# Paged keys turned by VectorE and pages gathered by SyncE in a two-layer attention kernel

## The chip, the cores and the metric

The kernel runs on one core of one Trainium2 chip. The metric is the device time of one execution in microseconds (us), here the median of three runs.

## The reference

Eight sequences (B=8) of 128 tokens, width 512, go through four residual steps. Layer 0: a windowed attention on x times an adapter matrix chosen by sequence, then a routed low-rank network. Layer 1: attention 1, causal with an alibi bias, on gated x; then attention 2 on the result, with a paged key and value cache, and a quantised two-matrix network on its output. What matters is attention 2:

```python
kc = k_cache[block_table].reshape(bsz, L, HK, D)      # 16 pages of 32 tokens, L=512
vc = v_cache[block_table].reshape(bsz, L, HK, D)
k_all = jnp.concatenate([kc, k], axis=1)              # k: normed and rotated, own 128 tokens
v_all = jnp.concatenate([vc, v], axis=1)
scores = jnp.einsum('bqhd,bkhd->bhqk', q, k_all) * SCALE
scores = jnp.where(valid[:, None, None, :], scores, -1e+30)
probs = jax.nn.softmax(scores, axis=-1)
o = jnp.einsum('bhqk,bkhd->bqhd', probs, v_all)
return jnp.einsum('bse,de->bsd', o.reshape(bsz, seqlen, HQ * D), Wo)
...
h = _dyn_quant_linear(_layernorm(attn2, gamma, beta), w1, b1)   # rows to 127 steps
out = x + _dyn_quant_linear(gelu(h), w3, b3)
```

There are 32 query heads in 8 key/value groups, head width 128; block_table and the cache lengths are inputs. All is float32; the cache holds 64 pages of 32 tokens x 8 groups x 128.

## The kernel before

Every engine's order is written out by hand, and semaphores tie the engines. Layer 0 goes sequence by sequence. Each attention of layer 1 has 64 items (ITEMS): for each of 8 groups g (four query heads, one key/value head) the 8 sequences b. Float32 products are done as three products of a high and a low part: ScalarE copies the high part (rounded), VectorE or GpSimd subtracts to get the low.

An item of attention 2 (step(i) of each engine). TensorE: scores of four heads (L1629, L1632) into two-bank pairs, the next item's key and value projection (project_kv, L1580), the transposes of the next item's four cached key tiles (turn_cached_k, L1589, bank 3), the output projection of the item before (project_out, L1674), the five transposed probability chunks (turn_probs, L1647) and their products with the values (weigh, L1662), and between them in quarters the query projection of the item after next (project_q, L1566), and the turned queries and key of the next (L1598, L1604). VectorE: four row maxima from the scores (row_max, L1991), the low part of the output (lo_of_o, L2013), two normalisations, the rotation of the next item's queries (spread_q, L1935 to L1939, and join_q, L1945) and key, then low parts of probabilities (L2007), cached keys (lo_of_cached_k, L1976), queries and key. ScalarE: exponentials, high parts, the squares of the query projection (q_squares, L2344). GpSimd: low part of the cached values (L2531), norm factors, and eight indirect DMAs per item, four 128x128 tiles of keys (L2517) and four of values (L2525), with row numbers made at the start (dve_positions, rows).

project_out of an item waits for the four row maxima of the next and for lo_of_o; row_max(0) frees bank 0 for the scores of head 3. Items with b=0 also split output weights (L1927), those with b=5 and b=6 the next group's query, key and value weights (L1922).

SyncE's queue (sp_layer0, sp_attentions) issues all other loads in order: in layer 0 one adapter per sequence, in attention 1 for each g the query/key/value weights, the output weights, in g=3 to 6 two stores of finished quantised weights (keep_units), and in g=2 to 5 two loads of rows of the quantised network's weights (load_units, L1322). VectorE takes those rows (unit_steps, L1895) as the first thing after the row maxima of items 10, 12, 18, 20, 26, 28, 34 and 36 (UNIT_ITEM), both loads of a pair being waited for at the first:

```python
            def unit_steps(n):
                dve.wait_ge(s_wn, 32 * (n // 2 + 1))
                row_steps(unit_step[:, n:n + 1], unit_inv[:, n:n + 1], unit_rows[n % 2])
```

After item 56 (LAST) the quantised network of each finished sequence is worked into the last items; quantised_end does the rest.

## Time and profile before

| | |
|---|---|
| median of 3 runs | 2039.4 us (2039.14 to 2040.28) |
| profiled execution | 2048.39 us, its span 2046.6 us |
| TensorE busy | 1990.2 us, 97% |
| VectorE busy | 1533.6 us, 75% |
| ScalarE busy | 1323.5 us, 65% |
| GpSimd busy | 801.8 us, 39%, of it 507.1 in 512 indirect DMAs (976 and 1005 ns each) |
| mean granted TensorE clock | 0.995 of full speed |

Layer 0 goes to about 300 us, attention 1 to 890 us, attention 2 to 2018 us, the rest is the quantised end. Busy time of TensorE overstates its work, as its products are pipelined; the starts of its instructions are what to read. The profiled execution is one run, longer than the median by 9.0 us.

### The profile page before, as it was taken

The page shows a single profiled execution, that of the slowest core. Times are in us where ns is not written, and L with a number is a line of the kernel's source. Part 1 is how long each engine was busy: PE and PEld are TensorE (multiplying, and loading weights), DVE is VectorE, ACT ScalarE, POOL GpSimd, SP SyncE. Part 2 cuts the span into 40 slices and gives each one's busy share as a digit, 9 for nine tenths or more (in the row PEclk, how much of TensorE's full clock was granted, in tenths as well). Part 3 has the DMA queues.
Part 4 walks back from the last instruction along what each step waited for, and adds up shares of the span by engine and source line. Part 5 has one row for each costly group of instructions (what it writes and reads, how often), then busy time and mean ns, then how long its engine had stood idle before and what let it go on. Part 6 is the DMA issues. An engine that isn't in the chain of part 4 may idle for free.

```text
span 2046.6 us, 35827 instructions
## 1 busy us (share of the span) xinstructions
PE 1990.2 (97%) x12449; PEld 1696.5 (83%) x12456; DVE 1533.6 (75%) x3383; ACT 1323.5 (65%) x3796; POOL 801.8 (39%) x797
## 2 busy tenths in 40 slices
PE   6999999999999999999999999999999999999986
PEld 5778677888888888888888888888888888888873
DVE  6777764556666555687887888878878888888997
ACT  4676763545554554566776777767767777677785
POOL 3200015100000000056666666666666666666662
PEclk9999999999999999999999999999999999999998
DMA  7301101101201110121111111211111111112000
GB/s 259 98 28 48 53 1 73 62 32 37 68 32 51 43 53 1 58 78 32 62 53 31 62 51 31 82 32 53 61 32 62 53 32 63 53 32 83 26 28 36
DMA packets 45010, 108.60 MB, mean 53 GB/s; under 512 B 15634, under 2 KB 21010, under 8 KB 40354
## 3 DMA queue, kind: packets, MB, share of 16 engines
q1 hardware_dynamic: 28450, 72.74, 10.3%
q0 software_dynamic: 16384, 33.59, 5.6%
q8 instruction: 102, 1.67, 0.3%
q14 instruction: 74, 0.61, 0.1%
HBM read 103.14 MB, written 3.15 MB: 52 GB/s over the span
## 4 chain that ended last, share of the span: by engine, by line
PE 90%; DVE 5%; ACT 3%; issue 1%; DMA 1%; SPq 0%; DVEq 0%; ACTq 0%
PE PS L1662 10%; PE PS L1487 9%; PE PS L1430 9%; PE PS L1674 8%; PE PS L1566 8%; PE PS L1629 7%; PE PS L1647 7%; PE PS L1580 4%; PE PS L1443 4%; PE PS L1632 3%; PE PS L342 3%; PE PS L1458 3%; PE PS L1473 2%; PE PS L498 1%; PE PS L1465 1%; PE PS L1589 1%
## 5 line engine op out<-in xcount | busy, mean ns | idle before, releaser
L2517 POOL DMA_INDIRECT kcache<-in_kcache,rows x256 | 249.9, 976 | 533.4 <-DVE x_res L1818 462.4
L2525 POOL DMA_INDIRECT vcache<-in_vcache,rows x256 | 257.2, 1005 | 124.2 <-issue 58.4
L1991 DVE CUSTOM_DVE_ANT_0 pr<-PS,ffn_weights,sm 128x640 f32<-128x640 f32 x256 | 224.6, 885 | 88.6 <-PE PS L1632 88.6
L2007 DVE TENSOR_TENSOR prT_lo<-PS,prT_hi 128x512 fp32r<-128x512 f32 x320 | 209.2, 685 | 46.1 <-ACT prT_hi L2387 41.8
L2376 ACT ACTIVATE pr<-pr,sm 128x640 f32<-128x640 f32 x256 | 212.3, 831 | 40.1 <-DVE sm L1991 40.0
L2387 ACT ACTIVATE prT_hi<-PS 128x512 fp32r<-128x512 f32 x320 | 178.9, 597 | 78.5 <-PE PS L1647 67.3
L1647 PE MATMUL PS<-consts,pr 128*128 128x128 f32 x1280 | 174.0, 273 | 2.7 <-DVE prT_lo L2007 1.6
L1647 PEld LDWEIGHTS PS<-consts,pr 128*128 128x128 f32 x1280 | 149.7, 141 | 28.8 <-issue 3.7
L2531 POOL TENSOR_TENSOR vcached_lo<-vcache,vcached_hi 128x512 fp32r<-128x512 f32 x64 | 83.2, 1300 | 228.8 <-ACT vcached_hi L2359 228.6
L1629 PE MATMUL PS<-kT_hi,qT_hi 128*128 128x320 f32 x512 | 154.5, 310 | 2.2 <-DVE sm L1991 1.3
L1629 PE MATMUL PS<-kT_lo,qT_hi 128*128 128x320 f32 x512 | 154.1, 309 | 0.0
L2381 ACT ACTIVATE pr<-pr,sm 128x640 f32<-128x640 f32 x128 | 99.3, 824 | 29.1 <-issue 25.8
L1566 PE MATMUL PS<-w_qkv_hi,xT_hi 128*128 128x512 f32 x256 | 117.5, 459 | 0.0
L1632 PE MATMUL PS<-kT_hi,qT_lo 128*128 128x320 f32 x512 | 116.6, 309 | 0.0
L2255 ACT ACTIVATE oT_hi<-PS 128x512 fp32r<-128x512 f32 x64 | 38.2, 597 | 116.7 <-PE PS L1473 116.7
L1430 PE MATMUL PS<-xT_hi,w_qkv_hi 128*128 128x512 f32 x256 | 110.4, 431 | 0.9 <-DVE xT_lo L1777 0.6
L1662 PE MATMUL PS<-prT_hi,vcached_hi 128*128 128x512 f32 x256 | 108.1, 422 | 2.8 <-DVE prT_lo L2007 2.1
L1674 PE MATMUL PS<-w_out_hi,oT_hi 128*128 128x512 f32 x256 | 106.8, 417 | 3.4 <-DVE oT_lo L2013 3.3
L2244 ACT ACTIVATE pr<-pr,sm 128x128 f32<-128x128 f32 x256 | 99.1, 392 | 6.1 <-DVE sm L1804 6.1
L1487 PE MATMUL PS<-w_out_hi,oT_hi 128*128 128x512 f32 x256 | 101.9, 398 | 0.2 <-DVE oT_lo L1832 0.2
L1629 PEld LDWEIGHTS PS<-kT_hi,qT_hi 128*128 128x128 f32 x512 | 96.1, 188 | 6.8 <-issue 2.5
L1566 PE MATMUL PS<-w_qkv_hi,xT_lo 128*128 128x512 f32 x256 | 101.4, 396 | 0.0
(319 smaller groups left out, 6173.3 us busy)
## 6 DMA issues: line engine op xcount, KB each, us to landing
arena<-in_wqkv SPq DMA_DIRECT2D x16, 1536.0 KB, 6.3
arena<-in_wo SPq DMA_DIRECT2D x16, 1024.0 KB, 5.4
arena<-in_wcT SPq DMA_DIRECT2D x8, 1024.0 KB, 6.6
kcache<-in_kcache,rows POOLq DMA_INDIRECT x256
vcache<-in_vcache,rows POOLq DMA_INDIRECT x256
arena<-in_xT SPq DMA_DIRECT2D x8, 256.0 KB, 8.2
x_res<-in_x SPq DMA_DIRECT2D x1, 2048.0 KB, 13.4
ffn_weights<-in_alibi SPq DMA_DIRECT2D x2, 1024.0 KB, 6.9
```

Of the source, the lines that this page charges most:

```text
L1430: mm = pe.matmul(bank(HEAD_BANK[n] if n < 2 * GH else 1), w_qkv[c][:, k, r * P:(r + 1) * P], (x_hi, x_lo)[a][:, k, GH * half:GH * (half + ...
L1487: mm = pe.matmul(bank(0 if last else 5), o2[a][:, h, :], w_out[c][:, h, :], start=(h == 0 and j == 0), stop=(h == GH - 1 and j == 2))
L1566: mm = pe.matmul(bank(7), (x_hi, x_lo)[a][:, k, b, :], w_qkv[c][:, k, 0:GH * HD], start=(k == 0 and j == 0), stop=(k == KT - 1 and j == 2))
L1629: pe.matmul(bank(SCORE_BANK[h] + half, HALF), qT2[0][:, h, :], kT2[c][:, half * HALF:(half + 1) * HALF], start=(c == 0), stop=False)
L1647: mm = pe.transpose(bank(4 + n % 2, P, h * P), pr2[:, h, c * P:(c + 1) * P], ident)
L1662: mm = pe.matmul(bank(6), v[a], prT2[e][:, n % 3, :, :].rearrange("p h n -> p (h n)"), start=(c == 0 and j == 0), stop=(c == CHUNKS and j ...
L1674: mm = pe.matmul(bank(0), o2[a][:, h, :], w_out[c][:, h, :], start=(h == 0 and j == 0), stop=(h == GH - 1 and j == 2))
L1991: dve.tensor_tensor_reduce(pr2[:, h, :].rearrange("p (a n) -> p a n", a=2), PS[:, SCORE_BANK[h]:SCORE_BANK[h] + 2, 0:HALF], keymask[:, b, ...
L2007: dve.tensor_tensor(prT2[1][:, n % 3, :, :].rearrange("p h n -> p (h n)"), bank(4 + n % 2), prT2[0][:, n % 3, :, :].rearrange("p h n -> p ...
L2376: act.activation(pr2[:, h, :], pr2[:, h, :], ACT.Exp, bias=nm2[:, h:h + 1], scale=-1.0, accum_out=rs2[:, h:h + 1]).then_inc(a2_ex, 1)
L2517: pool.indirect_dma_start(out=kcache[:, c, :], out_offset=None, in_=T["kcache"], in_offset=bass.IndirectOffsetOnAxis(ap=rows[:, g, b, c:c ...
L2525: pool.indirect_dma_start(out=vcache[:, c, :], out_offset=None, in_=T["vcache"], in_offset=bass.IndirectOffsetOnAxis(ap=rows[:, g, b, c:c ...
```

## The change

The pages of both caches are first copied, whole and in the order of the block table, into two DRAM tensors (kpages, vpages) by SyncE, one register load and two DMAs of 128 KB per page, 13 pages after each adapter of sequences 3 to 7 and 9 pages in each g=1 to 7 of attention 1. In attention 2 SyncE then loads each item's keys with four DMAs, each taking a quarter of the head width as pieces of 32 numbers, so that VectorE's transpose of 32x32 blocks gives the keys turned; values come with one DMA. TensorE's transposes of keys go. ScalarE's high part of the keys moves behind the third probability chunk, the low part goes to GpSimd. spread_q of the next item moves ahead of the row maxima, and the first quarter of the query projection ahead of the output projection. turn_hidden waits for a row maximum instead of the keys' low part. At the end sequence 6's dequantisation, steps and gelu move ahead and TensorE gets extra products that write a bank nobody reads (stay_warm). The weight loads of attention 2 are put between key and value loads. Page row numbers and positions on VectorE go; GpSimd makes the positions.

```diff
@@ -183,7 +180,7 @@
             kT2 = [sb2(f"kT2_{part}", [P, NKEY], F32R) for part in ("hi", "lo")]
-            kcache = sb2("kcache", [P, CHUNKS, HD])
+            kcache = sb2("kcache", [P, CACHED])
             vcache = sb2("vcache", [P, CHUNKS, HD])
@@ -207,6 +204,7 @@
         consts0 = area(22528, NCONST0)
+        kraw = cst["iota"]
         cst.update({n: consts0[:, a:b] for n, (a, b) in CONST0_COLS.items()})
@@ -276,9 +275,25 @@
         s_ym, s_g8 = sem("token_means"), sem("gate_ready")
-        NLOADF, NSETUP = 6, 10
+        NLOADF, NSETUP = 6, 7
...
         counted = {"dve": 0, "pool": 0}
+
+        kpages = nc.dram_tensor("gathered_k_pages", [B, SLOTS, PAGE, G, HD], F32).ap()
+        vpages = nc.dram_tensor("gathered_v_pages", [B, SLOTS, PAGE, G, HD], F32).ap()
+        L0_PAGES, A1_PAGES = 13, 9
+
+        def gather(sp, first, count):
+            if first == 0:
+                sp.wait_ge(s_setup, 16 * NSETUP)
+            for n in range(first, first + count):
+                b, s = n // SLOTS, n % SLOTS
+                at = (s % 4) * B * CHUNKS + b * CHUNKS + s // 4
+                page = sp.value_load(page_ids[0:1, at:at + 1], min_val=0, max_val=NPAGE - 1)
+                for kept, name in ((kpages, "kcache"), (vpages, "vcache")):
+                    sp.dma_start(kept[b, s:s + 1].rearrange("a t g d -> a t (g d)"),
+                                 T[name].rearrange("(a t g) d -> a t (g d)", a=NPAGE, g=G)[bass.ds(page, 1), :, :]
+                                 ).then_inc(s_gathered, 16)
@@ -314,6 +329,7 @@
                 adapter(b)
+                gather(sp, L0_PAGES * (b - 3), L0_PAGES)
@@ -1164,8 +1179,7 @@
         def sp_paged_inputs(sp):
-            for q in range(4):
-                sp.dma_start(page_i[q * 32:(q + 1) * 32, :], T["pages"][q, :].partition_broadcast(32)).then_inc(s_setup, 16)
+            sp.dma_start(page_ids[:], T["pages"].rearrange("q n -> (q n)").unsqueeze(0)).then_inc(s_setup, 16)
             sp.dma_start(clen_i[:], T["cache_len"].partition_broadcast(P)).then_inc(s_setup, 16)
@@ -1328,6 +1332,34 @@
+            def load_keys(n):
+                g, b = group_of(n)
+                if n == 0:
+                    sp.wait_ge(a2_mask, 2 * B)
+                    sp.wait_ge(a1_acc, ITEMS - B)
+                wait(sp, a2_kcT, n)
+                for j in range(4):
+                    sp.dma_start(kraw[j * PAGE:(j + 1) * PAGE, :].rearrange("t (s d) -> t s d", s=SLOTS),
+                                 kpages[b, :, :, g, j * PAGE:(j + 1) * PAGE].rearrange("s t d -> t s d")).then_inc(a2_kg, 16)
+
+            def load_values(n):
+                g, b = group_of(n)
+                if n == 0:
+                    sp.wait_ge(a1_sc, ITEMS)
+                wait(sp, a2_vcl, n)
+                sp.dma_start(vcache[:], vpages[b, :, :, g, :].rearrange("(c s) t d -> (s t) c d", c=CHUNKS)
+                             ).then_inc(a2_vg, 16)
+
+            def load_qkv_weights2(g):
+                wait(sp, a2_wl, QPARTS * g)
+                sp.dma_start(stage_qkv.rearrange("p t n -> p (t n)"),
+                             T["wqkv2"][g, :, :, :].rearrange("p t n -> p (t n)")).then_inc(a2_w, 16)
+
+            def load_out_weights2(g):
+                wait(sp, a2_wol, GH * g)
+                sp.dma_start(stage_out.rearrange("p h n -> p (h n)"),
+                             T["wo2"][g, :, :, :].rearrange("p h n -> p (h n)")).then_inc(a2_wo, 16)
+
             sp.wait_ge(s_prec, 3)
@@ -1341,6 +1373,8 @@
                     table(1)
+                if g:
+                    gather(sp, L0_PAGES * (B - 3) + A1_PAGES * (g - 1), A1_PAGES)
                 if 3 <= g < 7:
@@ -1350,23 +1384,37 @@
             sp.wait_ge(a1_wol, GH * G)
-            for g in range(G):
-                wait(sp, a2_wl, QPARTS * g)
-                sp.dma_start(stage_qkv.rearrange("p t n -> p (t n)"),
-                             T["wqkv2"][g, :, :, :].rearrange("p t n -> p (t n)")).then_inc(a2_w, 16)
-                wait(sp, a2_wol, GH * g)
-                sp.dma_start(stage_out.rearrange("p h n -> p (h n)"),
-                             T["wo2"][g, :, :, :].rearrange("p h n -> p (h n)")).then_inc(a2_wo, 16)
+            load_qkv_weights2(0)
+            load_out_weights2(0)
+            sp.wait_ge(s_gathered, 16 * 2 * B * SLOTS)
+            load_keys(0)
+            load_qkv_weights2(1)
+            load_values(0)
+            load_keys(1)
+            for i in range(LAST):
+                load_values(i + 1)
+                load_keys(i + 2)
+                g, b = group_of(i)
+                if b == 0:
+                    load_out_weights2(g + 1)
+                if b == B - 1 and g + 2 < G:
+                    load_qkv_weights2(g + 2)
...
             sp.dma_start(wrow.rearrange("p w n -> p (w n)"), step_kept.partition_broadcast(P)).then_inc(s_fi, 16)
+            load_values(LAST + 1)
+            load_keys(LAST + 2)
...
                 sp.dma_start(brow[:, w, :], T[bias].partition_broadcast(P)).then_inc(s_fi, 16)
+            for i in range(LAST + 1, ITEMS - 1):
+                load_values(i + 1)
+                if i + 2 < ITEMS:
+                    load_keys(i + 2)
@@ -1523,8 +1571,6 @@
                     project_q(0, (3,))
-                elif i == ITEMS - 2:
-                    turn_cached_k(0)
                 elif i == ITEMS - 1:
@@ -1581,14 +1627,6 @@
-            def turn_cached_k(n):
-                pe.wait_ge(a2_kg, 16 * CHUNKS * (n + 1))
-                if n == 0:
-                    pe.wait_ge(a1_kTc, ITEMS)
-                for c in range(CHUNKS):
-                    mm = pe.transpose(bank(3, P, c * P), kcache[:, c, :], ident)
-                mm.then_inc(a2_kcT, 1)
-
             def turn_q(n):
@@ -1677,9 +1717,11 @@
                 scores(i)
+                more = i + 2 < ITEMS
...
                     project_kv(i + 1)
-                    turn_cached_k(i + 1)
+                if more:
+                    project_q(i + 2, (0,))
                 if i >= 1:
@@ -1688,9 +1730,8 @@
                 turn_probs(i, 1)
-                more = i + 2 < ITEMS
                 if more:
-                    project_q(i + 2, (0, 1))
+                    project_q(i + 2, (1,))
                 if i + 1 < ITEMS:
@@ -1720,8 +1761,8 @@
                 pe.wait_ge(s_hq, n + 1)
-                if i is not None and i + 1 < ITEMS:
-                    pe.wait_ge(a2_kcl, i + 2)
+                if i is not None:
+                    pe.wait_ge(a2_max, 4 * i + 2)
                 else:
@@ -1746,6 +1787,10 @@
+            def stay_warm(n):
+                for _ in range(n):
+                    pe.matmul(bank(6), identb[:], wT16[:, 0, 0, :], start=True, stop=True)
+
             def quantised_end():
@@ -1753,12 +1798,19 @@
                 turn_hidden(5, 1)
+                stay_warm(2)
                 linear(5, 1, 4)
+                stay_warm(4)
                 turn_hidden(7, 0, bk=1)
+                stay_warm(2)
                 linear(7, 0, 0)
+                stay_warm(5)
                 turn_hidden(6, 1)
+                stay_warm(2)
                 linear(6, 1, 5)
+                stay_warm(4)
                 turn_hidden(7, 1)
+                stay_warm(2)
                 linear(7, 1, 7)
@@ -1850,6 +1902,7 @@
                     spread_q(0)
+                    turn_cached_k(0)
                 normalise1(i)
@@ -1971,9 +2019,10 @@
-            def lo_of_cached_k(n):
-                dve.wait_ge(a2_kch, n + 1)
-                dve.tensor_tensor(kT2[1][:, 0:CACHED], bank(3), kT2[0][:, 0:CACHED], ALU.subtract).then_inc(a2_kcl, 1)
+            def turn_cached_k(n):
+                dve.wait_ge(a2_kg, 16 * 4 * (n + 1))
+                wait(dve, a2_kcl, n)
+                dve.transpose(kcache[:], kraw).then_inc(a2_kcT, 1)
@@ -2026,6 +2075,8 @@
                 q = i - LAST
+                if more:
+                    spread_q(i + 1)
                 if q >= 4:
@@ -2039,7 +2090,7 @@
                 if more:
-                    rotate_q(i + 1)
+                    join_q(i + 1)
                     rotate_k(i + 1)
@@ -2049,7 +2100,7 @@
                     lo_of_own_v(i + 1)
-                    lo_of_cached_k(i + 1)
+                    turn_cached_k(i + 1)
                     norm_k(i + 1)
@@ -2167,14 +2218,14 @@
                 to_steps(5, 1)
+                dequantise1(6, 7)
...
                 quantise_hidden(7, 0)
-                dequantise1(6, 7)
+                hidden_steps(6, 1)
...
                 dequantise1(7, 0)
-                hidden_steps(6, 1)
                 hidden_steps(7, 1)
@@ -2354,14 +2405,15 @@
             def hi_of_cached_v(n):
-                act.wait_ge(a2_vg, 16 * CHUNKS * (n + 1))
+                act.wait_ge(a2_vg, 16 * (n + 1))
...
                 act.wait_ge(a2_kcT, n + 1)
-                act.activation(kT2[0][:, 0:CACHED], bank(3), ACT.Copy).then_inc(a2_kch, 1)
+                wait(act, a2_sc, 4 * n)
+                act.activation(kT2[0][:, 0:CACHED], kcache[:], ACT.Copy).then_inc(a2_kch, 1)
@@ -2414,8 +2466,6 @@
                     scale_hidden(q - 2, 0)
-                if more:
-                    hi_of_cached_k(i + 1)
                 if i + ITEMS - FROM_X < B:
@@ -2425,6 +2475,8 @@
                 hi_of_probs(i, 2)
+                if more:
+                    hi_of_cached_k(i + 1)
                 if new_out:
@@ -2491,12 +2543,12 @@
                 hidden_copy(5, 1)
+                gelu(6)
                 hidden_copy(7, 0, 1)
-                gelu(6)
-                gelu(7)
...
                 hidden_copy(6, 1)
+                gelu(7)
                 hidden_copy(7, 1)
@@ -2510,21 +2562,9 @@
-            def load_keys(n):
-                g, b = group_of(n)
-                wait(pool, a2_kcT, n)
-                for c in range(CHUNKS):
-                    pool.indirect_dma_start(out=kcache[:, c, :], out_offset=None, in_=T["kcache"],
-                                            in_offset=bass.IndirectOffsetOnAxis(ap=rows[:, g, b, c:c + 1], axis=0)
-                                            ).then_inc(a2_kg, 16)
-
-            def load_values(n, cs=range(CHUNKS)):
-                g, b = group_of(n)
-                wait(pool, a2_vcl, n)
-                for c in cs:
-                    pool.indirect_dma_start(out=vcache[:, c, :], out_offset=None, in_=T["vcache"],
-                                            in_offset=bass.IndirectOffsetOnAxis(ap=rows[:, g, b, c:c + 1], axis=0)
-                                            ).then_inc(a2_vg, 16)
+            def lo_of_cached_k(n):
+                pool.wait_ge(a2_kch, n + 1)
+                pool.tensor_tensor(kT2[1][:, 0:CACHED], kcache[:], kT2[0][:, 0:CACHED], ALU.subtract).then_inc(a2_kcl, 1)
@@ -2556,20 +2594,13 @@
-            pool.wait_ge(a1_acc, ITEMS - B)
-            load_keys(0)
-            pool.wait_ge(a1_sc, ITEMS)
-            load_values(0, (0, 1))
             factors(0)
-            load_values(0, (2, 3))
-            load_keys(1)
+            lo_of_cached_k(0)
...
                 if i + 1 < ITEMS:
-                    load_values(i + 1)
                     factors(i + 1)
-                if i + 2 < ITEMS:
-                    load_keys(i + 2)
+                    lo_of_cached_k(i + 1)
                 q = i - LAST
@@ -2577,9 +2608,13 @@
                     dequantise2(q - 4)
-                if q >= 1:
+                if q == 1:
+                    pool.wait_ge(s_fi, 16 * 6)
+                    bias_residual(7)
+                if 1 <= q < 7:
                     bias_residual(q - 1)
-            bias_residual(7)
+                if q == 6:
+                    bias_residual(6)
             root(7)
```

## Rows read from the trace of the kernel before

**Rows 1.** The page: the chain that ended last, shares of the span by engine.

```profile
PE 90%; DVE 5%; ACT 3%; issue 1%; DMA 1%; SPq 0%; DVEq 0%; ACTq 0%
```

**Rows 2.** Three items: us, then each engine's busy us (instructions), clock, DMA share, GB/s.

```profile
1272.13:1290.15 18.02, 17.86 (x105) 15.30 (x104) 16.56 (x36) 14.27 (x42) 10.36 (x11) 1.00 0.11 30
1324.48:1341.64 17.16, 17.16 (x105) 15.26 (x104) 14.37 (x34) 12.07 (x33) 10.97 (x11) 1.00 0.29 93
1934.30:1955.90 21.60, 20.01 (x120) 16.41 (x122) 19.93 (x50) 17.66 (x43) 15.34 (x15) 1.00 0.09 26
```

**Rows 3.** The chain in order of time, attention 2: start us, us, what.

```profile
1312.40 0.44 PE PS L1589 x4
```

**Rows 4.** Groups by line and shape: busy us, mean ns of one, idle before.

```profile
L1976 DVE TENSOR_TENSOR kT_lo<-PS,kT_hi 128x512 fp32r<-128x512 f32 x64 | 43.6, 681 | 0.0
...
L1922 DVE TENSOR_TENSOR w_qkv_lo<-arena,w_qkv_hi 128x1024 fp32r<-128x1024 f32 x8 | 9.8, 1225 | 2.0 <-ACT w_qkv_hi L2330 2.0
...
L2531 POOL TENSOR_TENSOR vcached_lo<-vcache,vcached_hi 128x512 fp32r<-128x512 f32 x64 | 83.2, 1300 | 228.8 <-ACT vcached_hi L2359 228.6 <-issue 0.2
```

**Rows 5.** Timeline, VectorE, items b=0: start us, us, engine, line, what [idle before].

```profile
1308.38 0.89 DVE L1991 CUSTOM_DVE_ANT_0 pr<-PS,ffn_weights,sm 128x640 f32<-128x640 f32 x1 [2.16 <-PE PS L1632]
...
1313.63 0.41 DVE L1935 TENSOR_TENSOR swapped<-PS,arena 128x256 f32<-128x256 f32 x1
...
1314.28 0.68 DVE L1939 TENSOR_TENSOR qk<-PS,arena 128x512 f32<-128x512 f32 x1
...
1323.32 1.89 DVE L1927 TENSOR_TENSOR w_out_lo<-arena,w_out_hi 128x512 fp32r<-128x512 f32 x3
```

**Rows 6.** Timeline, start of the item b=6 from 1272.13.

```profile
1273.20 0.21 ACT L2344 ACTIVATION_READ_ACCUMULATOR square<-PS 128x1 f32 x1
...
1273.21 0.89 DVE L1991 CUSTOM_DVE_ANT_0 pr<-PS,ffn_weights,sm 128x640 f32<-128x640 f32 x1
...
1276.65 0.69 DVE L2013 TENSOR_TENSOR oT_lo<-PS,oT_hi 128x512 fp32r<-128x512 f32 x1
...
1277.42 0.48 PE L1674 MATMUL PS<-w_out_hi,oT_hi 128*128 128x512 f32 x1
```

**Rows 7.** Timeline, SyncE's queue in layer 0.

```profile
25.90 2.55 SPq L309 DMA_DIRECT2D ffn_weights<-in_loraB  x1
...
61.61 0.37 SPq L314 DMA_DIRECT2D ffn_weights<-in_ffnB  x1
...
62.73 0.39 SPq L287 DMA_DIRECT2D arena<-in_wcT  x1
```

**Rows 8.** Timeline, quantisation rows loaded and used, groups g=2 and g=3.

```profile
394.51 0.91 SPq L1322 DMA_DIRECT2D arena<-in_w  x2
...
401.18 0.68 DVE L1895 TENSOR_REDUCE arena<-arena 128x1 f32<-128x512 f32 x1
...
468.85 1.56 SPq L1322 DMA_DIRECT2D arena<-in_w  x2
...
475.22 0.69 DVE L1895 TENSOR_REDUCE arena<-arena 128x1 f32<-128x512 f32 x1 [0.65 <-DMA arena<-in_w]
...
476.41 0.69 DVE L1813 TENSOR_TENSOR pr<-pr,sm 128x512 f32<-128x512 f32 x1
...
478.73 0.27 PE L1465 MATMUL PS<-consts,pr 128*128 128x128 f32 x1
```

**Rows 9.** Stretch at half clock in layer 0, columns as in rows 2.

```profile
42.41:45.82 3.41, 3.41 (x9) 2.64 (x8) 2.18 (x5) 1.94 (x4) 3.24 (x3) 0.50 0.01 2
```

**Rows 10.** Timeline, quantised end.

```profile
2037.16 0.43 DVE L2126 TENSOR_SCALAR arena<-ffn_weights 128x512 bf16<-128x512 f32 x1 [0.87 <-PE PS L1734]
...
2039.44 0.63 PE L1734 MATMUL PS<-identb,arena 128*128 128x128 bf16 x4
...
2040.76 1.89 PE L1745 MATMUL PS<-arena 128*128 128x512 bf16 x4 [0.69 <-ACT arena L2474]
```

**Rows 11.** DMA issues by line: count, KB each, median us to landing.

```profile
quantised_weights<-arena SPq DMA_DIRECT2D x8, 128.0 KB, 5.4
```

32 lines of the change are left out of this document (8 added, 24 removed).

## The prediction

> **What bounds the kernel now.** I read the page first: the span is 2046.6 us and TensorE is busy 97% of it. The chain that ended last is 90% TensorE [rows 1], so almost any instruction taken off TensorE should count, and so should any new wait of TensorE. Then I cut attention 2 into its items. The reader should see in [rows 2] that an ordinary item takes 17.16 us, with TensorE busy throughout, VectorE for 14.37 us even in an item that also splits weights, and GpSimd for 10.97. The item starts (first score product of each item) are 17.16 to 17.18 us apart in 48 of the first 57 items; seven, the seventh of each group (b=6), take 18.02, with TensorE waiting 0.8 us, and the first two are longer than that rule. The last seven items are different: the one from 1934.30 takes 21.60 us with VectorE busy 19.93 [rows 2]. There VectorE and ScalarE, with the quantised end's work between, set the pace. A measurement of this kernel can tell about 0.2% (4 us) from no change.
>
> **Cached keys.** Per item the change takes four TensorE transposes away. In the chain they cost 0.44 us, at 1312.40, between the k/v projection and the output projection [rows 3]. The 57 TensorE-bound items and the one transposed ahead in attention 1 give 58 x 0.44 = 25.5 us saved. On VectorE a subtraction of 0.681 us (128x512) leaves [rows 4] and a 32x32-block transpose of 128x512 in SBUF comes in. No row shows one. Bounds: 0.61 us (half of the 128x1024 subtraction's 1.225) and 1.225 itself, if it ran at half rate [rows 4]; I take 0.68, because the nearest row is an operation with as many elements, so VectorE's load stays. The Trainium skill (VectorE: DVE Perf Modes, section "The three transpose paths") gives 311 ns for 128x128 in bf16 and 390 ns for TensorE's; four times the first is an estimate of 1.24 us, and by it VectorE would have 0.56 us more per item, which an ordinary item's idle time holds. No row here shows a VectorE transpose to test it.
>
> The copy to kT_hi stays on ScalarE but moves behind the third probability chunk; its remainder moves to GpSimd, where the same shape takes 1.300 us [rows 4]. GpSimd loses eight indirect DMAs per item, about 1 us each, so it has room. The remainder would end some 2 us before the next item's scores: cost nothing; without that room, up to 1.3 us per item. The last seven items are bound elsewhere: I take -1.5 us for them, between -6 (the idle of VectorE filled by the query rotation) and +4 (seven transposes at 1.225).
>
> **Query rotation ahead of the row maxima.** It reads bank 7 after ScalarE's squares and takes 1.33 us (1313.63 to 1314.96) [rows 5]. In an ordinary item VectorE idles 2.16 us just there, before the row maximum at 1308.38 [rows 5], so the rotation is free, and its cover is this idle. In two items of each group the idle is gone. In the second item (b=1) VectorE is still splitting output weights until 1325.21 [rows 5]; rotation then ends at 1326.54, while the first row maximum started 1.08 us after the item's start, at 1325.56: 0.98 late. In b=6 the squares end at 1273.41 and the rotation at 1274.78, against a row maximum at 1273.21: 1.57 late [rows 6]. Who waits: the output projection, which needs all row maxima and oT_lo. It started at 1277.42; without transposes (-0.44) and with a quarter of the query projection (three products, 0.70) before it, it would be ready at 1277.68, and oT_lo ended at 1277.34 [rows 6]. So 0.34 us is slack: b=1 loses 0.64 x 8 = 5.1 us, b=6 loses 1.23 x 7 = 8.6. Against that the old 0.83 us stall of b=6 (5.8 us in all, later in the item, on late probability splits) may go, since the three products moved up leave more time before the probabilities. I take 8.6 - 5.8 = +2.8; between -5.8 and +8.6.
>
> **Pages copied in DRAM, and what SyncE does meanwhile.** This part decides. The portions stand on SyncE's queue: 13 pages after each of five adapters in layer 0, 9 in each of seven groups of attention 1. A page is one register load and two DMAs. No row shows such a page; its parts are shown. Between ffnB's issue ending at 61.98 and the next issue at 62.73 SyncE loads one id and computes an address: 0.75 us. Two ordinary issues take 0.91 us [rows 7, 8]. A page: 1.66 us; 13 pages 21.6; 9 pages 14.9. In layer 0 this is hidden: adapter b+1 is wanted some 30 us after it can now be issued. In attention 1 it is not. Each of groups g=2 to 5 issues, right after its output weights, the two rows of quantisation weights; now nine pages stand between. VectorE wants those rows almost at once: issued at 394.51, used at 401.18; issued at 468.85, used at 475.22 after 0.65 us of waiting for the DMA [rows 8]. VectorE takes unit_steps(n) first in items 10, 18, 26 and 34 and in order, so the normalisation of that item (476.41, 0.69) and TensorE's transposes (478.73) queue behind [rows 8]. Slack there is 478.73 - 477.10 = 1.6 us. So TensorE stalls 14.9 - 1.6 = 13.3 us four times, less the 1.0 us by which the first load was early: +52.2 us. Lower bound for a page 0.37 + 0.37 + 0.75 = 1.5 us (both issues as short as ffnB's): 4 x (13.4 - 1.6) - 1 = 46 us in all. Upper bound: with a full queue an issue took 2.55 us [rows 7]; at two of these a page is 5.9 us and the four stalls 206 us. I stay at the short end because the neighbouring issues, with data moving too, were short.
>
> A TensorE idle that long would lower its granted clock. A 3.4 us stretch at half clock (1.2 of 2.4 GHz) is to be seen at 42.41, following waits of TensorE for VectorE [rows 9]: four such cost 4 x 1.7 = +6.8 us; between 0 and twice that.
>
> Within the loop of attention 2 keys and values are loaded by SyncE; it waits there for a turned key, for GpSimd's remainder and at b=0 and b=7 for weight splits. Each load has most of an item before it is wanted. Cost nothing; see rival 2.
>
> **The ends.** At the start three of four page-id loads, a few VectorE operations of positions go: -1 us (0 to -3). At the end sequence 6's second product is put ahead and extra products keep the clock. h16 of (7,1) was written at 2037.16 to 2037.59 but TensorE took it up only at 2039.44, behind sequence 6; its product of 1.89 us ran at half clock [rows 10]. Gain 1.8 for the order, less 0.75 for a dequantisation now ahead of centre(7), plus about 1.7 for the clock if it holds: -2.8 us, between 0 and -5.
>
> **Sum.** 52.2 + 6.8 + 5.1 + 2.8 - 25.5 - 1.5 - 2.8 - 1.0 = +36.1 us. The profiled execution took 2048.39 us (span 2046.6), 9.0 above the median of 2039.4; the difference is carried to the median: 2075.5, say 2075 us.
>
> **Rival 1: SyncE is no obstacle (faster).** Then only the rest of the sum remains: -22.9, 2016.5 us. It needs nine pages in under about 7.3 us (4 x (7.3 - 1.6) = 22.9), 0.8 us per page. Against it: two issues alone are 0.74 to 0.91. For it: the register load might run ahead of the DMAs. Chance 0.15.
>
> **Rival 2: the key loads bound the loop (slower).** An item now reads 256 KB as 2048 pieces of 128 bytes in four DMAs. If the four landed one behind the other at 5.4 us each, as 128 KB writes of 256-byte pieces do [rows 11], an item would take 21.6 us: 64 x 4.9 = +310, about 2350 us. Against it: two such writes issued together overlap. [...] Chance 0.03.
>
> **Rival 3: pages slower than their issue (slower still).** A copy reads and writes DRAM, and loads behind it wait for its data. At 3 us a page the four stalls are 4 x 25.4 = 102 instead of 52: 2125 us. For it: the long issues at the start [rows 7]. Chance 0.13.
>
> The forecast has 0.69. **Chances and range.** Faster: rival 1 and a little of the forecast's lower tail, 0.16; within 0.2%: 0.03; slower 0.81. The forecast's own bounds (page 1.5 to 2 us, clock 0 to 13, b=6, last items) give about 2055 to 2095; to leave out no more than 2 in 10 I widen it to 2045 to 2110.
>
> **What would show it.** Items of attention 2 start 16.7 us apart with no transposes of kcache on TensorE; b=1 and b=6 lose about 0.6 and 1.2 us; VectorE's reduction of unit rows waits about 14 us for the DMA in items 10, 18, 26 and 34 and TensorE is idle there, with a half-clock stretch after. SyncE's pages stand 1.7 us apart. The prediction is wrong if those four waits are under 6 us, or the items of attention 2 don't shorten.

## The result and the profile after

| | median | runs |
|---|---|---|
| before, the same chip | 2039.84 us | 4 (2039.14 to 2040.55) |
| after | 2113.56 us | 4 (2111.46 to 2116.84) |
| ratio | 1.036 | 95% interval 1.0347 to 1.0372 |

73.7 us slower, where +36 was forecast and 2110 was the end of the range. The profiled execution has a span of 2110.0 us. First the page of after, the totals and the chain that ended last by engine:

```profile
span 2110.0 us, 36380 instructions
...
PE 1998.4 (95%) x12221; PEld 1676.2 (79%) x12221; DVE 1526.2 (72%) x3379; ACT 1330.2 (63%) x3796; POOL 397.8 (19%) x350
...
PE 77%; DVE 12%; SPq 4%; ACT 3%; issue 2%; DMA 1%; ACTq 0%; DVEq 0%
```

TensorE has fallen from 90% to 77% of the chain [rows 1]. SyncE's queue (SPq) now has 4% and VectorE 12%: there are new waits, of two kinds. The first is in the list of waits (engine line and tile, what it waited for: us, times, longest):

```profile
DVE arena L1947 <- DMA arena<-in_w: 61.5, 4, 16.2
...
PE PS L1513 <- DVE pr L1865: 52.2, 5, 13.7
```

VectorE waits four times some 15 us for the rows of quantisation weights, and TensorE behind it. The second of the four, on SyncE, then on VectorE and TensorE (start, duration):

```profile
480.27 0.33 SPq L1371 DMA_DIRECT2D arena<-in_wo  x1
481.36 0.51 SPq L294 DMA_DIRECT2D gathered_k_pages<-in_kcache  x1
481.97 0.53 SPq L294 DMA_DIRECT2D gathered_v_pages<-in_vcache  x1
483.26 0.49 SPq L294 DMA_DIRECT2D gathered_k_pages<-in_kcache  x1
...
485.13 0.49 SPq L294 DMA_DIRECT2D gathered_k_pages<-in_kcache  x1
...
497.71 0.53 SPq L294 DMA_DIRECT2D gathered_v_pages<-in_vcache  x1
498.29 1.12 SPq L1332 DMA_DIRECT2D quantised_weights<-arena  x2
499.46 1.02 SPq L1326 DMA_DIRECT2D arena<-in_w  x2
```

```profile
503.00 0.69 DVE L1947 TENSOR_REDUCE arena<-arena 128x1 f32<-128x512 f32 x1 [15.55 <-DMA arena<-in_w]
```

```profile
504.93 1.12 PE L1513 MATMUL PS<-consts,pr 128*128 128x128 f32 x4 [13.12 <-DVE pr L1865]
```

Nine pages, about 1.9 us apart, stand ahead of the rows. TensorE's granted clock in two-microsecond windows there (us, busy of PE, PEld, DVE, ACT, POOL, then the clock, DMA share, GB/s):

```profile
494.00:496.00 2.00, 0.00 (x0) 0.00 (x0) 0.00 (x0) 0.00 (x0) 0.00 (x0) 0.87 0.38 131
496.00:498.00 2.00, 0.00 (x0) 0.00 (x0) 0.00 (x0) 0.00 (x0) 0.00 (x0) 0.50 0.37 131
...
506.00:508.00 2.00, 2.00 (x11) 1.90 (x10) 1.29 (x3) 1.12 (x2) 0.00 (x0) 0.50 0.02 4
508.00:510.00 2.00, 2.00 (x8) 1.62 (x7) 1.29 (x2) 0.00 (x0) 0.00 (x0) 0.71 0.00 0
```

The clock falls to 0.50 (1.2 of 2.4 GHz) inside the stall and is still there for 4.2 us of work after it: the products start again at 504.93, and the mean of 0.71 in the last window puts the rise at 509.1.

The second kind stands in attention 2. One ordinary item of after, the chain through it (start, duration, what):

```profile
1178.26 0.58 PE PS L1669 x4
...
1181.77 1.42 PE PS L1626 x12
1183.19 0.70 PE PS L1612 x3
1183.89 2.80 PE PS L1714 x12
1186.69 0.87 PE PS L1687 x8
1187.56 0.70 PE PS L1612 x3
1188.26 0.44 PE PS L1636 x4
1188.70 0.80 PE PS L1702 x3
1189.50 0.44 PE PS L1687 x4
...
1191.44 0.44 PE PS L1687 x4
1191.88 0.04 issue
1191.91 0.66 PE PS L1687 x4
```

This answers to the item of [rows 3]. The four transposes of keys are gone, a quarter of the query projection (L1612 x3, 0.70) stands ahead of the output projection (L1714), and only 0.70 of it is left behind the first transposes of probabilities. The first weighting (L1702) takes 0.80 for its three products where the next takes 0.70 (and where the first one of units_both, below, takes 0.70), and four transposes (L1687) take 0.04 + 0.66 instead of 0.44. The item is 17.08 us long; before it was 17.16. I had expected 16.7.

The new VectorE transpose and GpSimd's remainder, grouped (us busy, mean ns):

```profile
L2567 POOL TENSOR_TENSOR kT_lo<-kcache,kT_hi 128x512 fp32r<-128x512 f32 x64 | 81.7, 1276 | 315.8 <-ACT kT_hi L2416 315.8
...
L2025 DVE STREAM_TRANSPOSE kcache<-consts 128x512 f32<-128x512 f32 x64 | 44.9, 701 | 0.0
```

### The profile page after: what moved, and what is told of

Read it like the earlier page. It is cut to its first block, busy times and chain, and to the rows that moved or that the text cites. A ratio compares the mean times of both kernels' runs of the same rounds, so it can differ in the third digit from the quotient of the medians.

```text
span 2110.0 us, 36380 instructions
## 1 busy us (share of the span) xinstructions
PE 1998.4 (95%) x12221; PEld 1676.2 (79%) x12221; DVE 1526.2 (72%) x3379; ACT 1330.2 (63%) x3796; POOL 397.8 (19%) x350
## 4 chain that ended last, share of the span: by engine, by line
PE 77%; DVE 12%; SPq 4%; ACT 3%; issue 2%; DMA 1%; ACTq 0%; DVEq 0%
PE PS L1714 8%; PE PS L1478 8%; PE PS L1535 7%; PE PS L1702 7%; PE PS L1612 7%; PE PS L1669 5%; PE PS L1687 5%; PE PS L1626 4%; PE PS L1491 3%; PE PS L358 3%; PE PS L1672 3%; PE PS L1506 2%; SPq L294 2%; PE PS L1521 2%; DVE prT_lo L2056 2%
## 5 line engine op out<-in xcount | busy, mean ns | idle before, releaser
L2439 ACT ACTIVATE prT_hi<-PS 128x512 fp32r<-128x512 f32 x320 | 184.4, 597 | 113.6 <-PE PS L1687 104.7
L2040 DVE CUSTOM_DVE_ANT_0 pr<-PS,ffn_weights,sm 128x640 f32<-128x640 f32 x256 | 220.3, 882 | 16.1 <-PE PS L1672 16.1
L1687 PE MATMUL PS<-consts,pr 128*128 128x128 f32 x1280 | 185.0, 275 | 4.1 <-DVE prT_lo L2056 2.1
L1687 PEld LDWEIGHTS PS<-consts,pr 128*128 128x128 f32 x1280 | 148.5, 141 | 42.2 <-DVE prT_lo L2056 19.2
L2578 POOL TENSOR_TENSOR norm_sums<-sm,pool_constants 128x5 f32<-128x5 f32 x64 | 27.3, 427 | 799.5 <-ACT square L2401 582.2
L1669 PE MATMUL PS<-kT_hi,qT_hi 128*128 128x320 f32 x512 | 156.4, 313 | 11.5 <-DVE sm L2040 9.9
L2567 POOL TENSOR_TENSOR kT_lo<-kcache,kT_hi 128x512 fp32r<-128x512 f32 x64 | 81.7, 1276 | 315.8 <-ACT kT_hi L2416 315.8
L1612 PE MATMUL PS<-w_qkv_hi,xT_hi 128*128 128x512 f32 x256 | 117.2, 458 | 3.4 <-DVE w_qkv_lo L1974 3.4
L1702 PE MATMUL PS<-prT_hi,vcached_hi 128*128 128x512 f32 x256 | 110.3, 431 | 1.6 <-DVE prT_lo L2056 1.6
L2301 ACT ACTIVATE prT_hi<-PS 128x512 fp32r<-128x512 f32 x64 | 38.2, 597 | 108.3 <-PE PS L1513 108.3
L1714 PE MATMUL PS<-w_out_hi,oT_hi 128*128 128x512 f32 x256 | 101.9, 398 | 3.7 <-DVE oT_lo L2062 3.7
L1535 PE MATMUL PS<-w_out_hi,oT_hi 128*128 128x512 f32 x256 | 102.3, 399 | 0.1
```

The source lines that it names most:

```text
L1535: mm = pe.matmul(bank(0 if last else 5), o2[a][:, h, :], w_out[c][:, h, :], start=(h == 0 and j == 0), stop=(h == GH - 1 and j == 2))
L1612: mm = pe.matmul(bank(7), (x_hi, x_lo)[a][:, k, b, :], w_qkv[c][:, k, 0:GH * HD], start=(k == 0 and j == 0), stop=(k == KT - 1 and j == 2))
L1669: pe.matmul(bank(SCORE_BANK[h] + half, HALF), qT2[0][:, h, :], kT2[c][:, half * HALF:(half + 1) * HALF], start=(c == 0), stop=False)
L1687: mm = pe.transpose(bank(4 + n % 2, P, h * P), pr2[:, h, c * P:(c + 1) * P], ident)
L1702: mm = pe.matmul(bank(6), v[a], prT2[e][:, n % 3, :, :].rearrange("p h n -> p (h n)"), start=(c == 0 and j == 0), stop=(c == CHUNKS and j ...
L1714: mm = pe.matmul(bank(0), o2[a][:, h, :], w_out[c][:, h, :], start=(h == 0 and j == 0), stop=(h == GH - 1 and j == 2))
```

## The experiments

Each kernel was timed beside before on one chip, but not all kernels on the same chip; ratios are to before, and between kernels of different chips the ratios compare better than the medians. The runs that share a chip are units_first, units_quarter, units_both and units_add; five_pages, add_thirds and weights_spread; add_weights, both_add, keys_on_tensor and before_end; end_cold, tail_on_tensor and mixed. For attention 2 I also list, from the timelines, the distance between the first products with qT_lo of successive items. "Ordinary" is b=2 to 5 and 7. The first two items are left out of b=0 and b=1. "First scores" is the start of the first such product.

| kernel | median | ratio (95%) | first scores | ordinary | b=6 | b=0 | b=1 | items 56 to 62 |
|---|---|---|---|---|---|---|---|---|
| before (profile) | 2039.84 | 1 | 891.41 | 17.16 | 18.00 | 17.17 | 17.16 | 137.6 |
| after | 2113.56 | 1.036 (1.0347-1.0372) | 951.92 | 17.08 | 18.42 | 17.26 | 17.54 | 141.1 |
| units_first | 2057.49 | 1.008 (1.0066-1.0093) | 893.81 | 17.08 | 18.44 | 17.25 | 17.53 | 141.1 |
| units_quarter | 2068.72 | 1.0132 (1.0116-1.0147) | 892.78 | 17.16 | 19.00 | 17.58 | 17.90 | 143.8 |
| units_both | 2049.29 | 1.0037 (1.0024-1.0051) | 892.76 | 17.17 | 18.13 | 17.57 | 17.19 | 136.9 |
| units_add | 2043.03 | 1.0013 (1.0004-1.0022) | 891.02 | 16.84 | 18.42 | 17.26 | 17.30 | 141.3 |
| five_pages | 2085.53 | 1.0202 (1.0185-1.0219) | 920.68 | 17.09 | 18.43 | 17.24 | 17.55 | 142.6 |
| add_thirds | 2066.11 | 1.0106 (1.0089-1.0123) | 894.56 | 17.12 | 19.03 | 17.84 | 17.59 | 144.5 |
| weights_spread | 2063.30 | 1.0095 (1.0078-1.0112) | 893.24 | 17.12 | 18.49 | 17.85 | 17.56 | 143.0 |
| add_weights | 2044.54 | 1.002 (1.0011-1.0029) | 891.68 | 16.84 | 17.88 | 17.76 | 17.39 | 142.0 |
| both_add | 2048.44 | 1.0042 (1.0029-1.0056) | 891.81 | 17.16 | 18.14 | 17.58 | 17.18 | 136.9 |
| keys_on_tensor | 2037.76 | 0.9987 (0.9978-0.9996) | 893.04 | 17.14 | 17.14 | 17.13 | 17.14 | 137.1 |
| before_end | 2036.48 | 0.9981 (0.9972-0.999) | 889.97 | 17.17 | 17.17 | 17.17 | 17.17 | 136.4 |
| end_cold | 2039.07 | 0.999 (0.9981-0.9999) | 891.50 | 17.17 | 17.17 | 17.17 | 17.17 | 136.4 |
| tail_on_tensor | 2039.20 | 0.9992 (0.9983-1.0001) | 892.48 | 16.84 | 18.43 | 17.26 | 17.29 | 137.0 |
| **mixed** | 2027.20 | **0.993** (0.9916-0.9943) | 892.47 | 16.83 | 17.13 | 17.13 | 17.13 | 137.0 |

### The stalls of attention 1

**units_first**: in each group of attention 1 the pages are issued last.

```diff
-                if g:
-                    gather(sp, L0_PAGES * (B - 3) + A1_PAGES * (g - 1), A1_PAGES)
                 if 3 <= g < 7:
                     keep_units(2 * g - 6)
                 if 2 <= g < 6:
                     load_units(2 * g - 4)
+                if g:
+                    gather(sp, L0_PAGES * (B - 3) + A1_PAGES * (g - 1), A1_PAGES)
```

> The changed kernel with one edit: in attention 1 SyncE issues the two rows of quantisation weights (and stores the finished ones) ahead of the group's nine pages instead of behind them. Theory A (the pages' issue time, 9 x 1.87 us, is what TensorE waits for): the four stalls (idle 11.9, 13.1, 13.1, 13.4 us in the trace of after, 51.4 in all) and the half-clock stretches behind them (about 10 us) go, and nothing else: first scores of attention 2 about 62 us earlier than after's 951, near 889, total 2113.6 - 62 = about 2052 us, still slower than before. Rival B (copying pages in DRAM while attention 1 runs costs something of its own, in transfers or in SyncE's other work): the stalls shrink but the total stays above 2060.

The first scores of attention 2 came at 893.81 instead of 951.92, 58.1 us earlier. TensorE's wait is gone, and VectorE's is down to three of 0.36 to 0.57 us, like the 0.65 of before [rows 8]. The total fell by 56 us to 2057.5. Theory A holds for the stalls.

The first scores are still 3.8 us later than in before_end (below), which copies no pages, but not all of this is the copies. The profiled executions differ in layer 0: units_first has 6.8 us at half clock there, after 3.4 us, before_end, units_add and five_pages none. The rows of units_first, the second from its quantised end (see there):

```profile
40.70:47.50 6.80, 6.80 (x21) 5.42 (x21) 3.51 (x8) 2.98 (x6) 6.39 (x6) 0.50 0.12 40
2013.60:2017.00 3.40, 3.40 (x10) 2.57 (x10) 0.21 (x2) 2.25 (x3) 0.00 (x0) 0.50 0.00 0
```

So I split at the start of the last output projection of layer 0 (L458, in before_end L442): 287.32 in after, 289.23 in units_first, 286.44 in units_add, 288.10 in before_end. From there to the first scores are 604.6 us in units_first and in units_add, 601.9 in before_end, before and end_cold, and 664.6 in after. By this the stalls with their half clock cost 60.0 us, and the copies without stalls 2.7. TensorE's four waits are 11.8, 13.1, 13.0 and 13.7 us, 51.8 in all (the expectation has 51.4); each stretch at half clock lasts another 3.2 to 4.7 us after the wait, 16.2 us in all, of which half, 8.1 us, is lost. Together that is 59.9.

**five_pages**: the order is left, and the portions are 15, 5, 5, 5, 5, 14, 14.

```diff
-        L0_PAGES, A1_PAGES = 13, 9
+        L0_PAGES, A1_PAGES = 13, (15, 5, 5, 5, 5, 14, 14)
```

> The changed kernel with the pages of attention 1 portioned 15, 5, 5, 5, 5, 14, 14 instead of seven times 9; the order of SyncE's work is kept, so five pages stand ahead of the rows of quantisation weights in groups 2 to 5. Theory A (TensorE's four stalls are the issue time of the pages ahead of these rows, 1.87 us each): each stall shrinks by 4 x 1.87 = 7.5 us, to about 5 us of idle time, and with it most of the half-clock stretches: 30 to 37 us under 2113.6, near 2080. Rival B (the stall is set by the transfers, the load of page numbers or anything else that doesn't grow with the pages ahead): less than 15 us faster.

The same two waits of this kernel:

```profile
DVE arena L1947 <- DMA arena<-in_w: 29.8, 4, 8.2
...
PE PS L1513 <- DVE pr L1865: 20.5, 5, 5.8
```

Sixteen pages fewer ahead of the rows took 31.7 us off both waits, 1.98 us a page. The median fell by 28 us, the ratio by 0.0158, which is 32 us. The stall is the issue time of the pages ahead of the rows.

### What the loop of attention 2 waits for

**units_quarter** puts the moved quarter back.

```diff
-                if more:
-                    project_q(i + 2, (0,))
                 if i >= 1:
                     project_out(i - 1)
...
-                    project_q(i + 2, (1,))
+                    project_q(i + 2, (0, 1))
```

> units_first, and the first quarter of the query projection of attention 2 stands again behind the second chunk of probability transposes, with the second quarter. Theory A (the quarter moved ahead took away the cover of TensorE's two waits for the remainders of the probabilities, 0.10 and 0.25 us per item, because the first transposes start 0.6 us later against the scores): the ordinary item falls from 17.08 to about 16.8 us; where VectorE rotates late (b=1 and b=6) the output projection has no cover and these items lose up to 0.7 us more. Over the loop 50 x 0.26 less 15 x 0.4: about 7 us faster than units_first. Rival B (the items are held by something else, VectorE's own total or the loads of keys): no item shortens, within 2 us of units_first.

A miss: 11 us slower than units_first, and no item shorter. The last seven items alone are 2.7 us longer. **units_both** takes the rotation back too, so that all is in the old order but for the transposes.

```diff
-                if more:
-                    spread_q(i + 1)
                 if q >= 4:
                     hidden_steps(q - 4, 1)
...
                 if more:
+                    spread_q(i + 1)
                     join_q(i + 1)
```

> units_quarter, and the query rotation stands again behind the reciprocals, as before the change: so the order of the work is the old one, without TensorE's four key transposes per item. Theory A (rotation ahead of the row maxima costs b=1 0.5 and b=6 1.3 us and gains nothing in other items): b=1 falls to the ordinary item, b=6 to about 17.6, the ordinary item is 16.8 us as in units_quarter, or up to 0.3 more where VectorE, which now rotates behind the reciprocals, starts the remainders of the probabilities late. Total 5 to 20 us faster than units_quarter, near 2030, faster than before. Rival B (the gain of the transposes is given back by VectorE, which has no idle left behind the reciprocals): ordinary item 17.1 us or more, total not faster than units_quarter.

The old order, without the 0.44 us of transposes, has an ordinary item of 17.13 to 17.19 us: as long as with them. So rival B holds for the item. The total did fall by 19.4 us against units_quarter, as theory A had it, but through b=1, b=6 and the last seven items (143.8 to 136.9). The chain through an ordinary item of units_both shows what took their place:

```profile
1066.24 0.58 PE PS L1669 x4
...
1069.81 0.87 DVE pr L2038
...
1070.69 0.61 DVE oT_lo L2060
...
1071.35 3.06 PE PS L1714 x12
1074.41 0.87 PE PS L1687 x8
```

The output projection waits for VectorE's four row maxima and the remainder of the attention output (oT_lo), which ends 0.04 us before the projection starts. The chain gives its twelve products 3.06 us here and 2.80 in the item of after above, but these pieces end where the profile models an end; the starts tell it more exactly. TensorE in units_both, then in after:

```profile
1070.89 0.28 PE L1626 MATMUL PS<-w_qkv_hi,xT_lo 128*128 128x256 f32 x1
1071.35 0.50 PE L1714 MATMUL PS<-w_out_hi,oT_hi 128*128 128x512 f32 x1 [0.18 <-DVE oT_lo L2060]
...
1074.25 1.04 PE L1687 MATMUL PS<-consts,pr 128*128 128x128 f32 x8
```

```profile
1183.72 0.40 PE L1714 MATMUL PS<-w_out_hi,oT_hi 128*128 128x512 f32 x1
...
1186.52 1.04 PE L1687 MATMUL PS<-consts,pr 128*128 128x128 f32 x8
```

The last k/v product is followed after 0.46 us; in after, where nothing is waited for, the next product starts 0.13 us behind it (1182.90 to 1183.03). That is 0.33 us of waiting. The twelve output products then take 2.90 us from start to start instead of 2.80. Together 0.43, the 0.44 of the transposes within rounding. The same is seen in the distance from the first product with qT_lo to the first output product: 4.71 us in before_end, with the four transposes between, 4.68 in units_both without them (medians of 28 items each). Only 0.03 us of slack stood behind the transposes. In the old order TensorE's transposes were filler in a place where it would have waited.

The comparison also gives the rotation its price: ahead of the row maxima it costs 0.87 us in b=6, 0.72 in b=1 and 6.9 in the last seven items (units_quarter against units_both) and nothing in ordinary items.

**both_add** is units_both with the edit of units_add (next), a test of where this order waits.

> units_both, and VectorE's addition of the output projection stands behind the third remainder of the probabilities, as in units_add. Theory A (in this order TensorE's wait is ahead of the output projection, for the row maxima and the remainder of the attention output, and the addition is not in that chain): ordinary item stays at 17.12 to 17.18 us, total within 3 us of units_both. Rival B (the addition ahead of the third remainder holds the item in this order too): ordinary item falls by 0.2 us or more, total 10 us or more faster.

17.16 us: theory A. VectorE's addition is not in the chain of the old order.

**keys_on_tensor** is units_both with TensorE's transposes of keys from copied pages, ScalarE's copy from PSUM and VectorE's remainder, all in the old places.

```diff
-                for j in range(4):
-                    sp.dma_start(kraw[j * PAGE:(j + 1) * PAGE, :].rearrange("t (s d) -> t s d", s=SLOTS),
-                                 kpages[b, :, :, g, j * PAGE:(j + 1) * PAGE].rearrange("s t d -> t s d")).then_inc(a2_kg, 16)
+                sp.dma_start(kcache[:], kpages[b, :, :, g, :].rearrange("(c s) t d -> (s t) c d", c=CHUNKS)
+                             ).then_inc(a2_kg, 16)
...
                     project_kv(i + 1)
+                    turn_cached_k(i + 1)
```

> units_both with the cached keys as before the change: loaded from the copied pages with keys on the partitions in one DMA, turned by four TensorE transposes per item, copied by ScalarE from PSUM, their remainder on VectorE. Against before it differs in the pages copied in DRAM, the loads by SyncE, the positions on GpSimd and the end. Theory A (in the old order TensorE's transposes only filled the time in which it would wait for the remainder of the attention output, so taking them away gains nothing): ordinary item 17.17 us as before, against 17.12 to 17.18 in units_both; total within 4 us of units_both. Rival B (the transposes cost their 0.44 us, something of the new loads or copies eats it): ordinary item 17.5 us or more, total 20 us or more above units_both.

Ordinary items 17.13 to 17.17: theory A for them. But the total is 11.5 us under units_both (10 by the ratios), which theory A had within 4. The difference is in b=6 (17.14 against 18.13) and b=0 (17.13 against 17.57), where weight splits share the queues: with VectorE's transposes the old order loses 1.4 us a group there.

**units_add** keeps the change's order and moves one VectorE operation.

```diff
-                if i:
-                    add(i - 1)
                 if more:
                     lo_of_q(i + 1)
                 lo_of_probs(i, 2)
+                if i:
+                    add(i - 1)
```

> units_first, with VectorE's addition of the output projection (0.68 us) put behind the third remainder of the probabilities instead of ahead of it; the quarter stays moved ahead. Theory A: what TensorE waits for before the fifth chunk of transposes (0.25 us) is VectorE's queue between the second and the third remainder, so 0.6 us less in this queue takes this wait away and leaves the 0.10 us before the first weighting: ordinary item 17.08 to 16.83 us, b=1 and b=6 not changed by more than that, total some 12 to 15 us under units_first. Rival B (that wait is for the chain transposes, ScalarE's copy, remainder, whatever else VectorE does): under 3 us.

16.84 us, as written, and 14.5 us off the total. VectorE's queue of after and of units_add, between the second and the third remainder of the probabilities:

```profile
1170.71 1.29 DVE L2056 TENSOR_TENSOR prT_lo<-PS,prT_hi 128x512 fp32r<-128x512 f32 x2 [1.84 <-ACT prT_hi L2439]
...
1172.90 0.68 DVE L2071 TENSOR_TENSOR ffn_weights<-PS,ffn_weights 128x512 f32<-128x512 f32 x1
1173.50 0.68 DVE L2029 TENSOR_TENSOR qT_lo<-PS,qT_hi 128x512 fp32r<-128x512 f32 x1
1174.10 0.68 DVE L2056 TENSOR_TENSOR prT_lo<-PS,prT_hi 128x512 fp32r<-128x512 f32 x1
```

```profile
1124.30 1.29 DVE L2056 TENSOR_TENSOR prT_lo<-PS,prT_hi 128x512 fp32r<-128x512 f32 x2 [1.84 <-ACT prT_hi L2439]
...
1126.48 0.68 DVE L2029 TENSOR_TENSOR qT_lo<-PS,qT_hi 128x512 fp32r<-128x512 f32 x1
1127.11 0.69 DVE L2056 TENSOR_TENSOR prT_lo<-PS,prT_hi 128x512 fp32r<-128x512 f32 x1
1127.72 0.68 DVE L2071 TENSOR_TENSOR ffn_weights<-PS,ffn_weights 128x512 f32<-128x512 f32 x1
```

From the start of the first remainder to the third are 3.39 us in after and 2.81 in units_add. VectorE has no gap in either. TensorE gets its 0.25 us back.

### Trials that failed

**add_thirds**: on top of units_add, the third quarter of the query projection ahead of the first weighting.

```diff
-                    project_q(i + 2, (1,))
+                    project_q(i + 2, (1, 2))
...
                 turn_probs(i, 2)
-                if more:
-                    project_q(i + 2, (2,))
```

> units_add, and the third quarter of the query projection moves from behind the third chunk of probability transposes to the second quarter, ahead of the first weighting. Theory A: the 0.10 us which TensorE still waits before the first weighting in every item is the chain transposes, ScalarE's copy, remainder, and 0.7 us more of products ahead of it cover it; the later chunks keep their remainders early enough: ordinary item 16.84 to about 16.74 us, 6 us in all. Rival B (the cover is missed behind the third chunk, the weighting of the second waits): ordinary item 16.84 or more.

Rival B, and by more than it says: 17.12 us an item, and 23 us slower than units_add by the medians, 19 by the ratios. The transposes of the third chunk come 0.7 us later behind the moved products, and VectorE now idles ahead of the third remainder:

```profile
1188.84 0.69 DVE L2054 TENSOR_TENSOR prT_lo<-PS,prT_hi 128x512 fp32r<-128x512 f32 x1 [0.44 <-ACT prT_hi L2437]
```

The same quarter of TensorE work is cover in one place and delay in the next. **weights_spread** is add_thirds with two of three splits of projection weights moved from the end of b=5 into b=6, on ScalarE and VectorE.

```diff
+                if new_weights:
+                    for part in (1, 2):
+                        lo_of_weights(g + 1, part)
                 lo_of_probs(i, 0)
...
                 if b == B - 3 and g < G - 1:
-                    for part in range(3):
-                        lo_of_weights(g + 1, part)
+                    lo_of_weights(g + 1, 0)
```

> add_thirds, and in the items before a new group only one of three splits of the projection weights (ScalarE's copy and VectorE's remainder, 0.63 us each on VectorE) stays behind the last probabilities of b=5; two move ahead of the first remainder of the probabilities of b=6, where VectorE idles 1.58 us. Theory A (b=6 takes 18.42 us because three splits and the rotation stand ahead of its row maxima): b=6 falls by 0.9 to 1.4 us, to about 17.2, total 6 to 9 us under add_thirds. Rival B (the splits are then late for the second and third quarter of the query projection and TensorE waits there): b=6 stays within 0.3 us of 18.4 or gets longer.

b=6 fell by 0.54 us against add_thirds, about half of what was expected, and the total by 2.8 us instead of 6 to 9. Since b=6 takes 19.03 us in add_thirds and not 18.42, its 18.49 is what rival B named. Whether TensorE waits where rival B says stays open. **add_weights** puts this on units_add, with the addition behind the fourth remainder in b=6 and b=0.

```diff
-                if i:
+                if i and not (new_weights or new_out):
                     add(i - 1)
...
                 lo_of_probs(i, 3)
+                if i and (new_weights or new_out):
+                    add(i - 1)
```

> units_add (the third quarter of the query projection stays where the change put it), with the two splits of projection weights moved as in weights_spread, and in b=6 and b=0, where VectorE splits a weight between the remainders, the addition of the output projection behind the fourth remainder instead of the third. Theory A: ordinary item 16.84 us as in units_add; b=6 from 18.42 to about 17.7 or less and b=0 from 17.26 to about 16.9: 6 to 8 us under units_add, under before by 2 to 5 us. Rival B (these items are held by ScalarE's part of the splits): less than 2 us under units_add.

b=6 fell to 17.88, but b=0 rose by 0.5 to 17.76, and the total came out no better than units_add. The addition in b=0 is better off early; why is open.

### The last eight items and the end

**before_end** is before with the new order of the end and the extra products alone; **end_cold** leaves the extra products out.

```diff
                 to_steps(5, 1)
+                dequantise1(6, 7)
                 centre(7)
...
                 turn_hidden(5, 1)
+                stay_warm(2)
                 linear(5, 1, 4)
```

> The kernel before with the change's new order of the quantised end and its extra products alone (their results are overwritten). Theory A: from the last item's scores to the end the changed kernel takes 44.9 us where before takes 49.1: this edit alone gives 3 to 4.5 us. Rival B (the shorter end comes from the later parts of the keys' change, VectorE and GpSimd being less busy there): under 1.5 us.

> before_end without the extra products: the new order of the end alone. Theory A (forecast's split: order 1.8 less 0.75, clock 1.7): 1.0 to 1.5 us of the 3.9 stay, so about 2039; the last products at half clock. Rival B (the order gives nearly all): within 0.7 us of before_end.

2036.48 and 2039.07: beside medians of before of 2040.39 and 2040.55 the edit gives 3.9 us and the order alone 1.5, so the extra products give 2.4. The two were timed on different chips, and the interval of end_cold's ratio (0.9981 to 0.9999) would allow the order 0.2 to 3.9 us, so this split is rough. The last products of end_cold, then of before_end:

```profile
2031.38 1.89 PE L1745 MATMUL PS<-arena 128*128 128x512 bf16 x4 [0.69 <-ACT arena L2474]
```

```profile
2028.71 1.04 PE L1745 MATMUL PS<-arena 128*128 128x512 bf16 x4 [0.26 <-ACT arena L2485]
```

The first answers to the last product of [rows 10], at half clock as there; the second ran at full clock. end_cold is at half clock for its last 15.0 us (2022.2 to 2037.2).

The extra products don't keep the clock in every execution. Of the fourteen profiled kernels that have them, six have no half clock in the quantised end, four have one stretch of 3.4 us and four, units_first among them (its row is above), have two. From the first scores of the last item to the end of the span these take 44.3 to 45.6 us, 45.6 to 46.2 us and 47.1 to 47.5 us.

**tail_on_tensor** is units_add with the old order and TensorE's transposes in the last eight items, and in the first two.

> units_add up to item 55, and in the last eight items the order of keys_on_tensor with TensorE's transposes. Theory A (the last seven items are held by VectorE and ScalarE; the new order, rotation first, costs them about 5 us): they fall from 124.1 us (units_add) to about 119 to 121 (before_end 119.2, keys_on_tensor 119.9), total 4 us under units_add, about 2039. Rival B (they are held by the quantised end's own chain whatever the keys do): within 1.5 us of units_add.

Items 56 to 62 fell from 141.3 to 137.0 us: the new order with VectorE's transposes costs 4.3 us there. It is the order and not the transposes, since units_both, with VectorE's transposes in the old order, takes 136.9.

### The version that beats both

**mixed**: each item turns the next item's keys on the engine that has room. Items b=2, 3, 4, 5 and 7 are as in units_add, the others as in keys_on_tensor; both kinds load into the same buffer and count on the same semaphores.

```diff
+        def by_vector(i):
+            g, b = divmod(i, B)
+            return 2 <= i < LAST and b in (2, 3, 4, 5, 7)
...
-                if more:
+                if more and by_vector(i):
                     project_q(i + 2, (0,))
```

> units_add in the items b=2, 3, 4, 5 and 7 of groups 0 to 6 (35 items or so); in b=0, 1, 6, in the first two and in the last eight items everything as in keys_on_tensor: TensorE turns the keys, rotation behind the reciprocals, quarter behind the transposes, addition ahead of the third remainder. Theory A (VectorE's transposes and the new order gain 0.3 us in items without weight splits and lose in the others): 16.84 us in the first kind, 17.15 in the second, 10 us under keys_on_tensor's 2037.8: about 2028, ratio to before 0.993 to 0.995. Rival B (the two orders don't fit together: each change of order costs a wait of its own, or the gain of 0.3 needs the item before in the same order): ordinary items over 17.0 or b=0, b=6 over 17.6, total not under 2034.

2027.20 us, ratio 0.993: 13 us under before and 86 under after, every kind of item as expected. So taking the transposes off TensorE is worth 0.3 us in 35 items, and only with the quarter, the rotation and the addition in their new places. No run has the new order with TensorE's transposes, so that the new places alone don't give the 0.3 is argued: in an ordinary item of before_end TensorE has no idle time that a new order could remove.

### What the profile of before held that its runs did not

**before_again** is before, profiled once more.

> The kernel before, unchanged, profiled once more on the chip of the other runs. The profile of before had a span of 2046.6 us, its timed runs elsewhere 2036.7 to 2041.0. Theory A: that profiled execution was a slow one, a new one has a span near 2037 and the 10 us are in attention 1 or ahead of it, since items of attention 2 in the changed kernels are as long as their sums say. Rival B: being profiled costs the kernel before some 8 us: span near 2046 again, with ordinary items of 17.16 us.

A span of 2045.6 us beside spans of 2040.9 to 2044.3 in the timed runs on that chip. Its b=6 items are 17.45 to 17.86 us and its first 18.73; in before_end and end_cold, which have the same loop, they are 17.17 and 17.55. The numbers are those of rival B (span near 2046, ordinary items of 17.17), but beside the other spans on that chip this one is only 1.3 to 4.7 us longer, not 8. Ordinary items and attention 1 are the same in all, and what a profiled execution of before had extra were those b=6 stalls (5.8 us in the first profile) and the first item's 1.2. The timed runs have no trace, so that they lack these stalls is argued from their time alone. I use before_end's loop as the undisturbed one below.

## Why the prediction was wrong, point by point

The ledger against the undisturbed loop, in spans, the end against the profile of before. Measured sums to +73.0, beside +73.7 of the medians:

| part | forecast | measured | from |
|---|---|---|---|
| four stalls and the clock after them | +59.0 | +60.0 | 664.60 - 604.58 |
| rest up to the first scores | -1.9 | +1.9 | 604.58 - 601.87 and 287.32 - 288.10 |
| items 0 to 55 | -16.7 | +10.4 | 972.6 - 962.2 |
| items 56 to 62 | -1.5 | +4.8 | 141.1 - 136.4 |
| end | -2.8 | -4.1 | 44.3 - 48.4 |

The first two rows are the distances from the last output projection of layer 0 to the first scores (the stalls section above), the second of them with what lies ahead of this projection (+2.7 and -0.8). The items from 0 to 55 make 27.1 of the 36.9 us by which the sum is off, the last seven another 6.3.

**The step that failed is "58 x 0.44 = 25.5 us saved" for the cached keys.** It took the share of TensorE in the chain as proof that a product taken away shortens the item. The chain says who was last, not by how much. Two things stood just behind: with 0.03 us of slack the remainder oT_lo for the output projection, and VectorE's queue for the probabilities. The prediction even had the first number: its slack, worked out for b=6, counted the 0.44 removed and the 0.70 moved in. But it charged the moved quarter nothing at the place it left. There the first weighting and the fifth chunk of transposes lost their cover, and 0.10 + 0.25 us of waiting came back. So the ordinary item gained 0.08 instead of 0.44, which over 56 items is 20 of the 27.1 us. units_both shows the other branch: without the moved quarter, all of the 0.44 is lost ahead of the output projection.

**b=1 and b=6.** The mechanism held (rotation behind weight splits, 0.72 and 0.87 us by units_quarter against units_both), the sizes less: b=1 lost 0.37 of the 0.64 forecast, b=6 lost 1.25 of 1.23. The credit of 5.8 us for the old stall in b=6 was wrong, since the undisturbed loop has no such stall. (The rotation's end in b=6 is 1274.74 by the prediction's own rows, not 1274.78; that changes nothing.) b=0 lost 0.09, and the first two items 1.2 and 0.6, which was not forecast.

**The last items** were counted -1.5 for what VectorE is spared; they lost 4.8. The bound of +4 was for transposes at half rate, and the transposes took 0.70 as assumed. The loss comes with the order, the rotation above all.

**The four stalls** were right in place, number and mechanism. That they were also right by 1 us in sum is luck: two errors cancel. The page took 1.87 us (483.26 to 485.13; 0.49 + 0.53 of issue and 0.85 between), not 1.66; but TensorE waited 51.8 us in the four, 12.9 each, of nine pages' 16.8, so the slack was 3.9, not 1.6. What is left of the 60.0 is 8.2 us of clock, where 6.8 was forecast.

**VectorE's transpose** took 0.701 us against 0.68 taken. The Trainium skill's figure for 128x128 in bf16 (VectorE: DVE Perf Modes, section "The three transpose paths"), times four, had made an estimate of 1.24 us; the trace disagrees, four times the area costs 0.70.

**The rivals.** Rival 1 (SyncE no obstacle) and rival 3 (3 us a page) are refuted by the period of 1.87. Rival 2: a load of keys landed in 2.2 us and the four issues take 1.90 together, and nothing in the loop of after waits for them.

```profile
consts<-gathered_k_pages SPq DMA_DIRECT2D x256, 64.0 KB, 2.2
vcache<-gathered_v_pages SPq DMA_DIRECT2D x64, 256.0 KB, 2.9
```

**The end** gave 4.1 where 2.8 was counted, in an execution of after without any half clock there; the edit alone gives 3.9 in the medians, of which the clock has about 2.4 (forecast 1.7) and the order 1.5 (1.05).

**Against the time of one execution.** The prediction worked from a profiled execution that was 9.0 us longer than the median, and put the difference that it found onto the median. After's profiled execution (2112.5 us) had no such surplus over its median. What before's had more were stalls that the median seems to lack, and the prediction counted 5.8 us of them as a gain of the change.

**What stays open.** Between the last output projection of layer 0 and the first scores every kernel with copied pages takes 2.5 to 2.7 us more than before_end, the stalls aside. It lies in attention 1, whose items are 9.14 us apart instead of 9.09, also in items during which no page is copied; the twelve k/v products take 1.42 us instead of 1.39. Why was not found. Why layer 0 and the quantised end have stretches at half clock in some executions and not in others is open too. Nor is it known why add_weights lost in b=0.

## What to carry to other kernels

A loop in which one engine is busy all the time can still be a ring of waits with a few tenths of slack. Before an instruction is counted as saved, find for each point where the engine takes up another's result how early that result is, and shorten the distance by what is removed and by what is moved away. A moved piece has two prices, at the place it leaves and at the place it enters, and a bulk issue put into a queue delays whatever stands behind it by its whole issue time. What reaches the busy engine is that time less its slack, here 12.9 of 16.8 us. Where items differ in load, let each take the variant that suits it: over the 63 items mixed gained 12 us (1086.7 against 1098.6) where the change for all items cost 15.

## What of the hardware was not expected

- TensorE's twelve output products took 2.90 us from start to start after a wait of 0.33 us and 2.80 without one: a short wait cost 0.10 us more than itself.
- A page (a number from SBUF into a register and two copies of 128 KB in DRAM) held SyncE's queue for 1.87 us, of which its two issues are 1.02; each copy landed in 2.4 to 2.6 us by the page of the profile, and the landing did not grow from the second page to the ninth of a portion (3.0 us for the key copy issued at 483.26, 2.3 for the one at 497.12), which speaks for the queue and not the data as what sets the pace.
- During a stall of 13.1 us the granted clock was 1.00, then 0.87, then 0.50, and 0.50 for 4.2 us of work after it. In the end of before_end products of no use (21 in all, in seven places) kept it at 1.00, where it was 0.50 for the last 15.0 us of end_cold without them; in eight of the fourteen kernels with them it still fell to 0.50 for 3.4 us once or twice.
- VectorE's transpose of 128x512 in 32x32 blocks, float32 and SBUF to SBUF, took 699 to 703 ns in 64 of 64 cases.
